# An attention stage: normalised rows moved from VectorE to ScalarE, places moved behind the next division

## The reference, cut to what matters

```
x = x + attention(layernorm(x))
x = x + experts(layernorm(x))
x = x + mixer(layernorm(x))
x = x + experts(layernorm(x))

attention: q, k, v = split(x @ Wqkv.T + b); q, k = rope(rmsnorm(q)), rope(rmsnorm(k))
           state = sum over rows of v (and 1) times relu(k), by head
           out = rmsnorm((relu(q) @ state / (relu(q) @ sums + 1e-6)) @ Wout.T + b)
experts:   the two best of 8 experts per row by a router; each expert is
           silu(x @ W1a) * (x @ W1b), then @ W2; the two results weighed by their gates
```

## Time and profile before

| | us |
|---|---|
| median of 3 runs (lowest, highest) | 1095.58 (1095.22, 1096.97) |
| the profiled execution, its own time | 1094.39 |
| its span, first to last instruction | 1092.5 |

### The profile page before, as it was taken

One profiled execution on the slowest core, in us unless ns is written; L12 is line 12 of the kernel. 1 busy time (PEld: TensorE's weight loads), 2 busy tenths in 40 slices (PEclk: granted clock), 3 DMA queues, 4 the chain that ended last, 5 costly groups with the idle time before them and its releaser, 6 DMA issues.

```text
span 1092.5 us, 19253 instructions
## 1 busy us (share of the span) xinstructions
PE 805.5 (74%) x4480; PEld 648.4 (59%) x4481; DVE 708.1 (65%) x2600; ACT 573.4 (52%) x1588; POOL 748.8 (69%) x1091
## 2 busy tenths in 40 slices
PE   3687787876419999999855676555751399999991
PEld 2466667765408999998623344323441399999881
DVE  4588898885524454454568888888854155666665
ACT  2786676662204434335578888888840143433430
POOL 2007776675755888887802589898888388888884
PEclk9788887786559999999878887778855699999996
DMA  7023222222245565566312231331114355789885
GB/s 197 20 59 88 82 77 66 87 73 70 80 130 159 178 189 184 184 189 197 102 58 77 87 111 38 102 104 51 54 59 129 85 181 186 240 265 293 282 248 158
DMA packets 159975, 142.67 MB, mean 131 GB/s; under 512 B 17539, under 2 KB 132876, under 8 KB 159792
## 3 DMA queue, kind: packets, MB, share of 16 engines
q1 hardware_dynamic: 121744, 70.98, 23.5%
q10 hardware_dynamic: 20448, 37.23, 10.5%
q0 software_dynamic: 17728, 33.88, 9.0%
HBM read 93.47 MB, written 50.37 MB: 132 GB/s over the span
## 4 chain that ended last, share of the span: by engine, by line
PE 41%; POOL 17%; DVE 14%; ACT 12%; issue 11%; DMA 3%; DVEq 0%; POOLq 0%; SPq 0%; ACTq 0%; another core or an unknown queue 0%
PE banks L1059 14%; POOL queue_dram L557 8%; PE banks L1079 7%; POOL result_dram L570 6%; PE banks L935 4%; POOL spacer L545 3%; PE banks L961 3%; DVE stats L1233 3%; PE banks L949 2%; ACT hmix L655 2%; PE banks L1067 2%; PE banks L1114 2%; ACT qkv L753 2%; PE banks L989 2%; PE banks L1115 2%
## 5 line engine op out<-in xcount | busy, mean ns | idle before, releaser
L557 POOL DMA_INDIRECT queue_dram<-hffn,place_i x256 | 297.5, 1162 | 169.8 <-remote 119.4
L570 POOL DMA_INDIRECT result_dram<-ytile,result_row x284 | 280.6, 988 | 93.1 <-issue 39.6
L1059 PE MATMUL banks<-xt,tile_up 128*128 128x256 f32 x1136 | 271.8, 383 | 5.2 <-DVE gated L1412 5.2
L769 ACT ACTIVATE gated<-banks,tile_bias 128x256 f32<-128x256 f32 x284 | 119.0, 470 | 234.4 <-PE banks L1059 196.0
L1412 DVE SCALAR_TENSOR_TENSOR gated<-banks,tile_bias,gated 128x256 f32<-128x256 f32 x284 | 124.2, 479 | 157.1 <-ACT gated L769 156.4
L1059 PEld LDWEIGHTS banks<-xt,tile_up 128*128 128x128 f32 x1136 | 207.1, 192 | 28.8 <-issue 3.6
L1079 PE MATMUL banks<-wdown_sb,gated 128*128 x1136 | 149.9, 275 | 3.9 <-DVE ytile L1420 3.9
L1079 PEld LDWEIGHTS banks<-wdown_sb,gated 128*128 128x128 f32 x1136 | 138.2, 192 | 4.5 <-issue 4.3
L545 POOL MEMSET spacer<- 128x176 f32 x508 | 138.8, 273 | 0.2
L935 PE MATMUL banks<-k_sb,hmix 128*128 128x128 f32 x128 | 30.0, 380 | 98.7 <-ACT hmix L655 69.9
L1067 PE MATMUL banks<-k_sb,xtile 128*128 128x128 f32 x284 | 55.4, 277 | 55.5 <-DMA xtile<-queue_dram 55.5
(11 more groups left out here) (213 smaller groups left out, 1579.7 us busy)
## 6 DMA issues: line engine op xcount, KB each, us to landing
tile_up<-w_up ACTq DMA_DIRECT2D x142, 256.0 KB
xtile<-queue_dram SPq DMA_DIRECT2D x142, 130.0 KB, 2.3
qkv<-result_dram SPq DMA_DIRECT2D x24, 512.0 KB, 5.4
x_dram<-xres SPq DMA_DIRECT2D x32, 256.0 KB, 2.8
result_dram<-ytile,result_row POOLq DMA_INDIRECT x284
xin<-x SPq DMA_DIRECT2D x16, 256.0 KB, 4.5
xold<-x SPq DMA_DIRECT2D x16, 256.0 KB, 4.1
queue_dram<-hffn,place_i POOLq DMA_INDIRECT x256, 2.4
```

Source lines behind the costliest of these rows:

```text
L557: nc.gpsimd.indirect_dma_start(queue_dram, bass.IndirectOffsetOnAxis(ap=place_i[s][:, at:at + 1], axis=0), hffn[s][c][:, j, :], None).then ...
L570: nc.gpsimd.indirect_dma_start(result_dram, bass.IndirectOffsetOnAxis(ap=result_row[i % SLOTS][:, h:h + 1], axis=0), ytile[i % SLOTS][:, h ...
L769: last = nc.scalar.activation(gated[i % GSLOTS][:, h, :], ps_up[i % 2][:, h, :], ACT.Silu, bias=tile_bias[i % STEP][:, h:h + 1])
L1059: last = nc.tensor.matmul(ps_up[i % 2][:, h, :], tile_up[i % WSLOTS][:, h * P:(h + 1) * P], xt[i % 2][:], start=True, stop=True)
```

## The change

Three edits, all in the attention stage, and no other work is added or left out:

- The rows for the experts are normalised by ACT (eight `Identity` activations with a per-row scale and bias) instead of by DVE (eight tensor-scalar operations). DVE makes the bias (`shift2`) with two small operations behind the state. On ACT the eight stand between `empty_qkv` of tiles 0, 1 and of tiles 2 to 7; before, three tiles were emptied ahead of the second inverse deviations.
- ACT's `inverse_deviations` of `ahead` stand between the key half and the query half of `scale_relu` of half 1, instead of behind both.
- DVE's `place` of a batch moves from the end of its round to behind the next round's `divide`. The last batch's place stays where it was.

```
 ACT
-                    scale_relu(1, turned)
-                if ahead is not None:
-                    for c in both:
-                        inverse_deviations(c, ahead, var_ready, moment, rstd, rstd_ready)
+                    scale_relu(1, turned, deviations_ahead)
...
-                    empty_qkv(ahead, range(0, 3))
+                    empty_qkv(ahead, range(0, 2))
                 if done is not None:
                     for c in both:
                         inverse_deviations(c, done, var2_ready, moment2, rstd2, rstd2_ready)
+                if done is not None:
+                    for c in both:
+                        act.wait_ge(queued[s][c], queued_by(before))
+                        normalise(c, scale2_ready, done, xres, rstd2, shift2, hffn[s], h2_ready)
                 if ahead is not None:
-                    empty_qkv(ahead, range(3, BT))
+                    empty_qkv(ahead, range(2, BT))
 DVE
                 if done is not None:
                     divide(done)
+                if placed is not None:
+                    place(placed, FIRST, 1 - s)
                 if turned is not None:
                     rotate(1, turned)
...
                 if done is not None:
                     residual(done)
-                    normalise_for_experts(done, s, before)
...
+                if done is not None:
+                    scales_for_experts(done)
                 if ahead is not None:
                     rotate(0, ahead)
                 if done is not None:
-                    choose(done, FIRST, s)
+                    choose(done, FIRST, s, before)
                     begin()
-                    place(done, FIRST, s)
```

More of the change, by code:

```diff
@@ L687, in out_norms, with scale_relu @@
                 nc.scalar.activation(out_rstd[c][:], out_sum[c][:], ACT.Abs_reciprocal_sqrt, bias=rms_eps[:, 0:1], scale=1.0 / D).then_inc(outrstd_ready[c], 1)
-            def scale_relu(c, m):
+            def scale_relu(c, m, between=lambda: None):
                 act.wait_ge(rotated_ready[c], m)
@@ L697, in scale_relu, with attention, deviations_ahead @@
                     last.then_inc(ready, 1)
-            def attention(done, turned, ahead):
+                    if half:
+                        between()
+            def attention(done, turned, ahead, s=0, before=0):
                 both = range(HALVES)
+                def deviations_ahead():
+                    if ahead is not None:
+                        for c in both:
+                            inverse_deviations(c, ahead, var_ready, moment, rstd, rstd_ready)
                 begin()
@@ L709, in attention @@
                     copy_turned(0, turned, qf_turned, ps_turn[0], qf_t[0][:], qft_ready)
-                    scale_relu(1, turned)
-                if ahead is not None:
-                    for c in both:
-                        inverse_deviations(c, ahead, var_ready, moment, rstd, rstd_ready)
+                    scale_relu(1, turned, deviations_ahead)
+                else:
+                    deviations_ahead()
                 if done is not None:
@@ L863, in normalise_routed @@
                 act.wait_ge(queued[s][c], queued_by(before))
-                normalise(c, scale2_ready, b, xres, rstd2, shift2, hffn[s], h2_ready)
+                normalise(c, scale2_ready, b + BATCH, xres, rstd2, shift2, hffn[s], h2_ready)
             def route(b, s, before, between):
@@ L906, in _ @@
             attention(None, 1, 2)
[L907 to L910, removed]
+            with act.Fori(0, BATCH // 2 - 1) as n:
+                attention(n * 2 + 1, n * 2 + 2, n * 2 + 3, 1, n)
+                attention(n * 2 + 2, n * 2 + 3, n * 2 + 4, 0, n)
+            attention(BATCH - 1, BATCH, None, 1, BATCH // 2 - 1)
+            attention(BATCH, None, None, 0, BATCH // 2 - 1)
             plan(FIRST)
@@ L1263, in normalise_in @@
                 normalise(m, xin, moment, rstd_ready, rstd, hmix, h_ready)
[L1265 to L1268, removed]
             def choose(m, f, s, before=0):
@@ L1273, in choose @@
                 for c in both:
-                    if f == SECOND:
-                        dve.wait_ge(queued[s][c], queued_by(before))
+                    dve.wait_ge(queued[s][c], queued_by(before))
                     nc.vector.tensor_copy(hffn[s][c][:, :, D], k_sb[:, bass.ds(at + (K_TOKEN + c * TPC), TPC)])
@@ L1511, in residual, with attention @@
                 moments(xres, stats2, moment2, var2_ready)
-            def attention(done, turned, ahead, s=0, before=0):
+            def attention(done, turned, ahead, s=0, before=0, placed=None):
                 if done is not None:
                     divide(done)
+                if placed is not None:
+                    place(placed, FIRST, 1 - s)
                 if turned is not None:
@@ L1652, in _ @@
             begin()
[L1653 to L1657, removed]
+            attention(1, 2, 3, 1, 0)
+            with dve.Fori(0, BATCH // 2 - 2) as n:
+                attention(n * 2 + 2, n * 2 + 3, n * 2 + 4, 0, n, placed=n * 2 + 1)
+                attention(n * 2 + 3, n * 2 + 4, n * 2 + 5, 1, n + 1, placed=n * 2 + 2)
+            attention(BATCH - 2, BATCH - 1, BATCH, 0, BATCH // 2 - 2, placed=BATCH - 3)
+            attention(BATCH - 1, BATCH, None, 1, BATCH // 2 - 1, placed=BATCH - 2)
+            attention(BATCH, None, None, 0, BATCH // 2 - 1, placed=BATCH - 1)
+            place(BATCH, FIRST, 0)
             plan(FIRST)
```

## The result

| | before | with the change |
|---|---|---|
| median of the runs shown with the result (lowest, highest), us | 1095.4 (1092.9, 1097.0) | 1122.05 (1120.8, 1122.6) |
| span of the profiled execution, us | 1092.5 | 1120.6 |
| mean granted TensorE clock | 0.839 | 0.830 |

The ratio is 1.0246, with a 95% interval of 1.0228 to 1.0264: slower by 27 us, where +24 was forecast and 1106 to 1131 given as the range.

What follows compares the result with a forecast made beforehand. A loop through several engines, none full, was taken to bound the 30.1 us round; 2.2 + 21.5 + 0.8 + 1.4 - 0.6 = +25.3 on 1094.4 gave 1119.7, stated as 1119 us, range 1106 to 1131.

Steps and rivals of the forecast that it cites:

- Place behind the division: From last read to next division: the place leaves the path, -2.05 us a round; the rotation behind it comes 1.4 later.
- Norms: ACT's output norms behind the rotation and moments: start at 11.3 us behind the division, not 8.9, so +2.4.
- The hole: PE standing ahead of the fifth QKV tile (tile 4) while ACT waits and normalises rows: 4.3 us, adding 3.9 a round.
- one of my signs: Sign that the forecast is right: ACT idle ahead of `rstd2` with only two tiles emptied; no size given.
- ran fast: In the trace before the change, PE's QKV block ran fast; the clock's fall came late, in reads and division wait.
- Rival 1, the clock: PE's clock falls in the hole every round: 3.9 x 6 = +23 on top, 1142 us; chance 0.10.
- Rivals 2 and 3: Rival 2: ACT's slack fills the hole ahead of tile 4, only late norms stay, 1097 us, chance 0.06.
- rival 3: DVE is the bound and ACT has slack: 2.05 us given back seven times, -14, 1081 us; chance 0.04.
- hole theory: ACT's wait and eight activations between QKV tiles 1 and 2 make the loss; the other two edits nearly cancel.

Runs made afterwards that it cites:

- between_dev_back: The changed kernel with row activations one at a time between emptying QKV tiles 3 to 7, deviations back behind both halves of scale_relu: 1109.98 us, ratio 1.0133.
- rows_late: The changed kernel with three tiles emptied ahead of the second deviations and the eight row activations behind all eight QKV tiles: ratio 1.0307, on another chip.

## Why the prediction was right, and where its terms were off

The parts, as ratios to the kernel before:

| rows on ACT | place moved | deviations between | kernel | ratio |
|---|---|---|---|---|
| | x | | place_only | 0.9906 |
| | | x | dev_only | 1.0020 |
| x | | | rows_only | 1.0263 |
| x | x | | dev_back | 1.0160 |
| | x | x | rows_back | 0.9954 |
| x | x | x | the change | 1.0246 |

Rows with the deviations and without the place was not run.

- **Place behind the division.** The term was -2.05 a round at its end, with 1.4 of delay behind it. Both showed: reads to division fell from 1.96 to 0.15 us in the mean of the six rounds, so by 1.8, and the rotation of half 1 ends at 7.4. Alone it is worth 8 us; the net of -2.05 and a delay that ACT's own work partly covers.
- **Norms.** Here a term was off. I said +2.4, from the round that starts at 86.47. Over the six rounds the norms before start at 8.9 to 9.7, 9.3 in the mean; with the change 11.2 in rounds 2 to 5. So it was +1.9. I had taken one of the two rounds with the earliest norms as the pattern. The key half before did not wait for the rotation at 6.0, as I had it, but for ACT's copy of the turned queries: that ended at 6.3 in those two rounds and at 6.6 to 7.1 in the other four, and the norms started 2.6 behind it in all six.
- **The hole.** Tile 4 started at 22.7 to 23.5 in rounds 2 to 6, for 22.9 forecast. The visible wait was less, 2.1 to 3.0 in these rounds and not 4.3, because tiles 0 and 1 ran at the low clock and filled it. One step did not hold, and one of my signs with it: ACT was to stand idle ahead of `rstd2`. It did so in the first round alone (0.91). In the other five the moments were there at 18.4 to 18.7, but ACT had emptied the slow tile 1 only at 18.5 to 19.5, and the normalising began at 19.05 to 19.9, not at 19.2. In the first round it began 0.5 behind the moments; by that, my estimate is that the slow tiles 0 and 1 cost 0.2 to 0.8 us in each of the five rounds. That the QKV block "ran fast" before is true of four rounds; in the first and fifth its first tiles took 1.6 us too.
- **Rival 1, the clock.** I gave it 3.9 a round and 1 in 10 that it comes whole. It came in part. The last four tiles took 5.9, 4.9, 5.0, 3.4, 3.4 and 5.0 us, 4.6 in the mean for 3.6 before: 1.0 a round. The scores kept to 1.95 in all six. Tile 4 itself, right behind the wait, had these rows in the second and fourth round (the third number from the right is the granted clock):

```profile
111.90:113.60 1.70, 1.65 (x3) 0.86 (x4) 1.29 (x2) 0.37 (x1) 1.53 (x3) 0.50 0.19 61
184.70:185.60 0.90, 0.84 (x3) 0.48 (x4) 0.48 (x1) 0.38 (x2) 0.90 (x2) 1.00 0.24 79
```

Over the six rounds its clock was 0.50, 0.50, 0.67, 1.00, 1.00 and 1.00, behind waits of 4.1, 2.5, 2.1, 2.95, 2.95 and 3.0. In the sixth the clock fell one tile later.

The rule of the Trainium skill ("TensorE: Matmul & The Clock Gate", section "HAM oscillation — how this bites in real kernels") that a wait between groups can send the array back to the low clock agrees with the first three rounds; in the other three tile 4 started at the full clock.

- **Sum.** For the six rounds I forecast 2.2 + 21.5 = +23.7 and measured +29.8: +2.2 in the first, as forecast, and +5.5 for +4.3 in the mean of the other five. By terms, in the mean of the six: tile 4 came 5.9 later, as much as the forecast had for the QKV block; the last four tiles took 1.0 more, where nothing was forecast; reads to division gave back 1.8 for 2.05; the way from the router turns to the last read was 0.2 shorter. So the forecast fell short by about what the last four tiles took.

  Outside these rounds I forecast +0.8, +1.4 and -0.6, together +1.6. Measured were 32.07 - 31.69 = +0.4 in the seventh round, -0.1 in the last (26.87 from the division of batch 8 to its place, before 27.0), -0.25 on the way in, and the 1.7 given back behind the last place, which I had not forecast and which no run explains: -1.7. In the last round the scores end 21.5 behind the division (before 21.7) though the normalising takes its 1.1 more, as the second moments are there at 13.5 and not at 14.8. The two errors, 6 us too few and 3 too many, have opposite signs. So the mechanism was right, and that 1119 came within 3 us of 1122 is in part luck.
- **Rivals 2 and 3.** `rows_back` and `place_only` show a gain such as rival 3 spoke of, though 5 to 10 us and not 14, and only once the rows are off ScalarE. DVE's 2.06 us less were worth nothing: it idled 3.9 us ahead of the rotation instead.

Of the hole theory one half is shown: the loss goes with the rows on ScalarE in both settings (+2.6% alone, +2.9% on top of the other two). That their position between tiles 1 and 2 makes the loss is not: the hole is where the time is seen in the changed kernel, but one at a time between the copies (`between_dev_back`), or behind all eight tiles (`rows_late`), the rows cost as much or nearly, now ahead of the router turns. What is shown is that 3.1 us more between the second moments and the scores on ScalarE cost 2.3 to 2.9%. The interaction of the deviations with the place is shown by its size (2 us alone, 9 in the changed kernel; 5 on top of the place), its split between the norms and the clock only by the timelines of single executions.

## What to carry to other kernels

Before work moves to an engine that looks idle, lay out in time what stands behind it in that engine's queue and who waits for it: ScalarE was less busy in a round than VectorE, PE and GpSimd, but three microseconds put between the second moments and the scores, where PE waits for it, cost 5 us a round. Cutting them into pieces closed the hole that was seen and gave back little of the time (1.0160 to 1.0133), since PE then waited further on. A step whose result is needed late, such as the place here, may go behind the next step of the critical loop, and was worth 0.6 to 1.0% by itself. When a round's pattern varies, take several rounds for the terms of a sum, not the tidiest one.

## What had not been expected

- One chip ran the kernel before in 1221.5 us, another two in 1095.6 and 1096.0. On it, ACT stood for up to 9.4 us with no releaser of the program in its trace, and PE, which waits for ACT's copy, for up to 13.8, in some rounds and not in others. The transfers had the same sizes. The cause is open. Ratios from that chip had intervals about twice as wide.
- How the granted clock lies over a round matters as much as its mean: 0.830 with the change and 0.839 before, yet the last four QKV tiles lost 1.0 us a round. With `rows_back` the mean was 0.85, and its reads from the second to the fifth round took 3.7 us, where before they took 3.7 to 6.4.
